# A hint on the loop's closing branch, and the second half's low parts moved between two score tiles

## The reference

```
q = x @ wq + x @ Aq @ Bq * 4 ;  k = x @ wk ;  v = x @ wv + x @ Av @ Bv * 4      (16 heads of 16)
q, k = rope(q), rope(k)
attn = softmax(causal(q k^T / 4)) ;  o = attn @ v
x1 = layernorm(x + o @ wo)
h  = gelu(butterfly_up(x1 @ W_exp + b_exp) + up_bias)        (1024 wide)
out = layernorm(x1 + butterfly_down(h) @ W_con + b_con + down_bias)
```

## Time and profile before

| | |
|---|---|
| median of three executions | 1196.34 us |
| the profiled execution, its own time | 1196.34 us |
| its span, first to last instruction | 1194.6 us |
| mean granted TensorE clock | 0.956 of full speed |
| TensorE matmul busy | 89% of the span |
| VectorE, ScalarE, GpSimd busy | 74%, 59%, 49% |

### The profile page before, as it was taken

The page is one execution under the profiler, slowest core; times in us unless marked ns, Lnnn a source line. Parts: engine busy times, 40 slices in busy tenths (PEclk is TensorE's granted clock), DMA queues, the critical chain, the costliest instruction groups (busy, mean ns, idle before and its releaser), DMA issues.

```text
span 1194.6 us, 28482 instructions
## 1 busy us (share of the span) xinstructions
PE 1062.5 (89%) x8974; PEld 791.1 (66%) x8974; DVE 884.0 (74%) x1946; ACT 705.6 (59%) x1097; POOL 584.4 (49%) x567
## 2 busy tenths in 40 slices
PE   4577789999998999989999899989999899998886
PEld 3454457768676777767777676767777676766675
DVE  6589957787887678767787777767787778777454
ACT  2176548475766648466675747466574747566523
POOL 5242425556473736447383646547283555634311
PEclk9687879999999999999999999989999999999999
DMA  7764453646464574646465464645556365643111
GB/s 264 160 197 108 163 116 112 179 120 198 107 198 115 159 179 135 170 104 187 103 215 128 146 173 119 188 105 181 127 184 159 114 178 120 205 93 102 65 37 36
DMA packets 95128, 171.62 MB, mean 144 GB/s; under 512 B 14872, under 2 KB 36120, under 8 KB 94944
## 3 DMA queue, kind: packets, MB, share of 16 engines
q1 hardware_dynamic: 93888, 166.53, 50.7%
q10 hardware_dynamic: 832, 1.83, 0.4%
q0 software_dynamic: 224, 1.04, 0.2%
HBM read 92.28 MB, written 77.07 MB: 142 GB/s over the span
## 4 chain that ended last, share of the span: by engine, by line
PE 66%; DVE 15%; issue 8%; DMA 5%; ACT 3%; POOL 2%; SPq 1%; DVEq 0%; POOLq 0%; ACTq 0%
PE ps_m L634 26%; PE ps_m L754 11%; PE ps_m L788 7%; PE ps_m L682 6%; PE ps_m L763 5%; DVE m_raw L995 4%; PE ps_m L793 4%; DVE g_lo L476 4%; PE ps_t L725 3%; PE ps_m L711 2%; ACT pT L867 2%; DVE x1T L1024 2%; DMA k_st<-qk_scr 1%; POOL o_c L1159 1%; DMA r_b<-r_scr 1%
## 5 line engine op out<-in xcount | busy, mean ns | idle before, releaser
L867 ACT ACTIVATE pT<-ps_t 128x512 f32<-128x512 f32 x640 | 330.2, 603 | 284.7 <-PE ps_t L725 284.3
L1146 POOL TENSOR_SCALAR_AFFINE_SELECT pT<-pT 128x512 f32<-128x512 f32 (+1 forms) x320 | 201.6, 634 | 390.4 <-ACT pT L867 388.7
L995 DVE TENSOR_REDUCE m_raw<-ps_m 128x1 f32<-128x512 f32 (+2 forms) x768 | 337.6, 502 | 33.4 <-PE ps_m L711 32.7
L682 PE MATMUL ps_m<-k_st,q_st 48*128 48x512 f32 (+3 forms) x1024 | 152.2, 352 | 43.9 <-DMA k_st<-qk_scr 19.4
L754 PE MATMUL ps_m<-pT,v_aug 128*32 128x512 f32 (+3 forms) x2048 | 159.0, 453 | 8.7 <-DVE m_raw L995 3.2
L634 PE MATMUL ps_m<-x1T,w_hi 128*128 128x512 f32 x512 | 155.5, 412 | 1.6 <-ACT x1T L891 1.0
L682 PEld LDWEIGHTS ps_m<-k_st,q_st 48*128 48x128 f32 x1024 | 88.8, 189 | 98.5 <-issue 61.8
L725 PE MATMUL ps_t<-q_st,k_st 50*128 50x512 f32 (+3 forms) x1024 | 123.8, 348 | 3.9 <-DMA q_st<-m_scr 2.3
L754 PEld LDWEIGHTS ps_m<-pT,v_aug 128*32 128x32 f32 x2048 | 59.6, 113 | 89.3 <-issue 80.8
L634 PEld LDWEIGHTS ps_m<-x1T,w_hi 128*128 128x128 f32 x512 | 97.9, 196 | 27.0 <-issue 2.2
L1041 DVE TENSOR_SCALAR gact<-ps_m,gbias 128x512 f32<-128x512 f32 x64 | 47.8, 748 | 66.7 <-PE ps_m L634 66.3
(11 more groups left out here) (119 smaller groups left out, 2096.2 us busy)
## 6 DMA issues: line engine op xcount, KB each, us to landing
qk_scr<-rot_hi SPq DMA_DIRECT2D x62, 512.0 KB, 3.6
q_st<-qk_scr SPq DMA_DIRECT2D x128, 192.0 KB, 4.4
k_st<-qk_scr SPq DMA_DIRECT2D x128, 192.0 KB, 4.8
qk_scr<-rot SPq DMA_DIRECT2D x32, 512.0 KB, 4.5
o_scr<-o_raw SPq DMA_DIRECT2D x64, 256.0 KB, 3.6
r_b<-in_xT SPq DMA_DIRECT2D x17, 512.0 KB, 5.5
o_c<-o_scr SPq DMA_DIRECT2D x32, 256.0 KB
r_b<-r_scr SPq DMA_DIRECT2D x32, 256.0 KB
```

The lines of the kernel that those rows point to most:

```text
L682: return pe.matmul(scores[r][:, off:off + (qt + 1) * P], q_st[rows, pr, qt * P:(qt + 1) * P], k_st[rows, pr, 0:(qt + 1) * P], start=start, ...
L867: act.activation(pT[:, slot, half * T:(half + 1) * T], ps_t[:, ST_BANK[2 * n + r], :], ACT.Exp, scale=SCALE).then_inc(exp_done, 1)
L995: ins = dve.tensor_reduce(m_raw[:, g % 2, r, u // 2, qt:qt + 1], scores[:, off:off + (qt + 1) * P], AX.X, ALU.max, negate=True)
L1146: pool.affine_select(out=v, in_=v, compare_op=ALU.is_ge, fill=0.0, base=0, pattern=pattern, channel_multiplier=-1).then_inc(mask_done, 1)
```

## The change

Two edits. The low parts LO 2 and LO 3 of batch i-2 move from the head of slot 3 to slot 2, between the two score tiles S12 and S13.

```
@@ early(p), p == 3
             gemm("V", i + 1, 1)
-            put("LO", i - 2, 2)
-            put("LO", i - 2, 3)
             put("RCP", i - 1, 1)
             put("REC", i - 1, 1)
@@ between(p)
-        if p == 6:
+        if p == 2:
+            put("LO", i - 2, 2)
+            put("LO", i - 2, 3)
+        elif p == 6:
             put("LNB", i - 1, 0)
             put("LNB", i - 1, 1)
@@ each
-            with eng.Fori(3, B - 2, 2) as i:
+            with nc.Fori(3, B - 2, 2, engines=bass.OrderedEngineSet([eng.engine]), hint_back_edge=True) as i:
@@ TensorE
-            with pe.Fori(3, B - 2, 2) as i:
+            with nc.Fori(3, B - 2, 2, engines=bass.OrderedEngineSet([pe.engine]), hint_back_edge=True) as i:
```

## The result

| | before | after |
|---|---|---|
| median | 1195.02 us (7 runs, 1193.22 to 1196.35) | 1204.21 us (7 runs, 1200.26 to 1206.86) |
| profiled execution, span | 1196.34, 1194.6 | 1205.0, 1203.2 |
| mean granted clock | 0.956 | 0.945 |

A forecast was written before the change was run, and what follows sets the result against it. TensorE, busy 89%, was taken to bound the kernel, losing time at taken back edges. Sum: 1196.3 - 26.8 (branch) + 0.8 + 8.5 (late reciprocal) = 1178.8 us; range 1160 to 1189.

The forecast's parts named there:

- The hint: TensorE's closing branch: five taken back edges lose 5.36 us each; removing this gives 26.8 us, with 0.8 added back.
- The exit: TensorE's branch falling through at loop end: stays at 83 ns; rival that it pays a fetch, 5.4 us once, chance 0.08.
- the stall did not move: Rival at TensorE's loop branch: the fetch is paid ahead of the branch on all six trips, 1210 us, chance 0.05.
- The low parts' own price: VectorE, low parts between S12 and S13: the pair takes 0.65 us longer each period beside GpSimd's line 460.
- The pair at 4.0: Line 476 on VectorE: the two low parts take about 4.0 us instead of 3.38.
- the reciprocal's 0.65: RCP on VectorE: starts 0.65 us later, at 617.45 instead of 616.80, some 6.6 us behind the maxima's start.
- line 793's 0.5: TensorE's wait at line 793 for VectorE's low parts: falls from 1.09 to near 0.5 us.
- The step that failed: At WO: TensorE's earlier arrival only lengthens its wait; RCP's 0.65 us delay moves WO equally, 13 times, plus 8.5 us.
- above 1.5: Sign for the low parts in the profile after: TensorE's wait at WO above 1.5 us, ordinary window near 66.2.
- The upper bound of 14 us: Low parts' worst case: they lose a whole GpSimd instruction more, 14 times 1.0 us.
- I cost both at nothing now and gain nothing by removing them: Branch stalls of VectorE (3.2 us) and SyncE (4.5 us): taken as hidden under queued or distant work, priced at zero.
- the hint does nothing: Rival at TensorE's branch: five stalls stay, only the low parts act, 1204.8 us; chance 0.12, of which 0.04 at 1196.

The follow-up runs named there:

- experiment 10: Kernel after with GpSimd's ROPE 1 moved behind its two masks, so the low parts meet no rotation: 1202.47 us, ratio 1.0074 against the kernel before.
- experiment 4: Kernel after with four extra matmul calls (8 matmuls, result unread) on TensorE ahead of WO's wait: 1184.55 us, ratio 0.9918 against the kernel before.
- experiments 8 and 9: Kernel before with the back-edge hint on TensorE's loop only: 1194.82 us; with it on TensorE's and SyncE's loops only: 1173.05 us.

## Why the prediction was wrong

**The hint** was right in kind and gave a quarter less than forecast. Forecast 26.8 less 0.8; the hint alone gives 1193.0 - 1173.6 = 19.4 us by medians. The branch is as forecast. But ten periods of its trace, from the WO at 355.36 to that at 1015.62 us, average 66.0 us and not 65.6, which is 5 us over twelve periods, one of 68.1 us among them in which WO waited for the reciprocals. That the stalls had given this chain slack which is now wanted back is my reading, not tested. The exit costs 88 ns, so it pays nothing that shows, the stall did not move, and the rule of the Trainium skill (Runtime: NRT & Kernel Launch, section "Instruction fetch mechanics") that prefetch is purely sequential would have put the kernel at 1204.8 for a reason that the 365 ns of the branch refute.

**The low parts' own price** was right. The pair at 4.0 was 4.13 (3.88 or 3.89 in every other period), the reciprocal's 0.65 was 6.69 - 5.95 = 0.74, line 793's 0.5 was 0.51. That GpSimd's rotations slow the pair was shown by experiment 10; this is where the rule that I weighed (the Trainium skill, SBUF — State Buffer, section "Who interferes with whom") gave the better sum, and the traces agree: 4.13 with two rotations, 3.38 with the end of one and a mask, 2.35 with neither, and the second rotation took 2.27 us beside the pair where it had taken 1.29. The reciprocals' delay by itself costs some 12 us where I summed 8.5: 0.74 and 0.21 us a period in place of 0.65.

**The step that failed** is this one: "A TensorE that comes 0.4 us earlier waits 0.4 us longer. RCP 0.65 us later moves WO 0.65 us later. Periods 2 to 14, 13 times 0.65: plus 8.5 us." Its lengths are nearly right. My own terms give a wait of 0.74 + 0.4 + 0.65 = 1.8 us, and I wrote "above 1.5" for it; 2.09 was measured. Then I priced that wait at its length. What it cost besides is the clock, for which the sum has no term: 1.6 to 1.7 us in the WO of a period, 18 to 20 us in all by experiment 4. The upper bound of 14 us was of the same kind, more of the same delay, and could not hold it. The evidence stood on the page that I had read: TensorE idle for 3.56 us and then a clock of 0.50, which I counted as part of the branch's price and did not take to be a property of idle stretches. The trace of the kernel before even has it at WO itself, at the first one, where the 2 us behind its start are granted 0.50:

```profile
149.68 6.44 PE L763 MATMUL ps_m<-wo,o_c 128*128 128x256 f32 x16 [3.05 <-POOL o_c L1159]
```

The reason that I gave for the earlier TensorE, that it gains nothing, was itself too kind: coming 0.4 us earlier to a wait that ends on another chain makes the idle stretch longer, and so it can cost.

**Two more that did not decide.** "I cost both at nothing now and gain nothing by removing them", on the other engines' stalls, named VectorE's 3.2 us as the most that could show. SyncE's is the one that counts: TensorE's hint gains nothing without it, 1194.8 against 1173.1 us with it (experiments 8 and 9; SyncE's alone was not tried). It was hidden only as long as TensorE stood beside it. And the chances: no case among mine was "the hint works and the time is 1204"; the rival "the hint does nothing" had 0.12, of which 0.08 lay at this number, by another way.

**Open.** Between 1.38 and 2.92 us of wait both clocks occur, so the length of the last wait alone does not decide; what else does, the short waits before it for one, was not tried. The hint alone gives 19.4 us where its forecast is 26, and only the 5 us of longer periods are placed. Why an unhinted branch costs SyncE 4.7 us and GpSimd 0.3 was not tried either.

## What to carry to other kernels

Price a wait of TensorE not at its length alone: look in the trace for the longest wait behind which the granted clock stays up, and count the matmuls that follow at the lower clock where an edit makes a wait longer than that; also where the edit only brings TensorE to the wait sooner. On a queue, put the step that starts a chain through DRAM ahead of work that nobody awaits yet, but not before its own input can be there. And when a stall is taken from the engine that bounds, look for the same stall on the engines that feed it, a DMA queue's above all, which had been hidden beside it.

## What had not been expected of the hardware

- Behind a wait of 2.1 us at WO the granted clock is 0.50 in the kernel after, and the sixteen matmuls behind it take 5.38 us instead of 3.69. Eight useless matmuls of 1.99 us in the wait make the program 20 us faster.
- The hinted taken branch costs 365 ns in the median where it cost 3.68 us, and the hint 31 to 41 ns in the median on each of the five engines; the exit is 88 ns, before 83.
- The same wait at WO, 1.4 to 2.0 us, now keeps the clock and now loses it within one execution. The kernel with most of its waits there, that with 512 columns of delay, spreads over 18 us in ten runs, the kernel before over 7 in nineteen.
